# A graph network with attention and mixture of experts, on one core: the one-hots of keys and locals of a tile in one VectorE instruction

## What is computed

```python
xn = _layernorm(x)
agg = segment_sum(xn[dst], src, num_segments=3125)      # 53125 edges
y = agg + w * xn
h = relu(relu(relu(y @ W1.T) @ W2.T) @ W3.T)            # 256 -> 64 -> 32 -> 256
graph = h + xn
q, k, v = heads(xn)                                     # 8 heads of 32; q, k = elu + 1
mix = (q @ (k.T @ v)) / max(q @ sum(k), 1e-6)           # linear attention, per head
x = x + graph + (mix @ Wproj.T + bproj)
x = x + moe(_layernorm(x))                              # 8 experts, top 2, gelu; adds its input too
```

## Time and profile before

| | us |
|---|---|
| median of 3 runs | 431.22 (428.87 to 433.67) |
| the profiled execution | 430.48 |
| its span, first to last instruction | 428.8 |

### The profile page before, as it was taken

One profiled execution on the slowest core, in us unless ns is written; L12 is line 12 of the kernel. 1 busy time (PEld: TensorE's weight loads), 2 busy tenths in 40 slices (PEclk: granted clock), 3 DMA queues, 4 the chain that ended last, 5 costly groups with the idle time before them and its releaser, 6 DMA issues.

```text
span 428.8 us, 10052 instructions
## 1 busy us (share of the span) xinstructions
PE 404.5 (94%) x3141; PEld 318.8 (74%) x3141; DVE 311.2 (73%) x785; ACT 265.8 (62%) x676; POOL 183.5 (43%) x298
## 2 busy tenths in 40 slices
PE   4989899997999999999999999978999999999995
PEld 1767678776677777777755667854999998988894
DVE  3688858967899999999727653667688887655553
ACT  1756655575788888888824614441776766666663
POOL 4058969246100010001091114464456565655655
PEclk9899999999999999999999987577999999999999
DMA  8927310006589999999997961124465665467651
GB/s 211 194 70 255 90 26 8 1 2 125 106 152 172 172 175 167 179 184 189 167 215 227 308 224 63 65 81 120 151 190 188 187 210 159 140 202 207 186 177 38
DMA packets 111827, 64.11 MB, mean 150 GB/s; under 512 B 87985, under 2 KB 102202, under 8 KB 111646
## 3 DMA queue, kind: packets, MB, share of 16 engines
q1 hardware_dynamic: 104590, 48.14, 51.0%
q0 software_dynamic: 6368, 14.47, 9.6%
q10 hardware_dynamic: 816, 0.85, 0.8%
HBM read 24.00 MB, written 21.44 MB: 106 GB/s over the span
## 4 chain that ended last, share of the span: by engine, by line
PE 52%; POOL 12%; issue 11%; DMA 10%; DVE 10%; ACT 3%; SPq 1%; POOLq 0%; DVEq 0%
PE bank L1432 9%; PE bank L1381 8%; PE bank L1475 6%; POOL xs_next L653 5%; PE bank L1346 4%; PE bank L1444 4%; DMA region_a<-xs_next 4%; PE bank L1355 3%; POOL out L660 3%; DMA out<-region_a 3%; PE bank L1612 2%; PE bank L1594 2%; PE bank L1454 2%; DMA xs_next<-region_a 2%; POOL region_a L648 2%
## 5 line engine op out<-in xcount | busy, mean ns | idle before, releaser
L725 ACT CAST region_a<-bank 128x500 bf16<-128x500 f32 (+1 forms) x119 | 70.0, 673 | 14.8 <-PE bank L1381 14.8
L1681 PE MATMUL bank<-region_a,region_c 128*128 128x128 f32 x496 | 65.6, 275 | 0.0
L1692 PE MATMUL bank<-region_c,region_a 128*128 128x256 f32 x248 | 64.0, 380 | 0.0
L1681 PEld LDWEIGHTS bank<-region_a,region_c 128*128 128x128 f32 x496 | 60.3, 191 | 0.1
L1142 DVE COPY region_c<-region_w 128x1026 f32 x62 | 43.5, 701 | 19.2 <-issue 17.7
L605 POOL COPY wide<-den 125x256 f32<-125x256 f32 x25 | 13.0, 518 | 100.6 <-DVE den L1057 100.6
L1381 PE MATMUL bank<-region_a 128*128 128x125 bf16 x625 | 52.9, 219 | 1.5 <-ACT region_a L725 1.4
L1381 PEld LDWEIGHTS bank<-region_a 128*128 128x128 bf16 x625 | 42.2, 101 | 13.6 <-ACT region_a L725 3.2
L989 DVE TENSOR_TENSOR region_a<-iota,keys 128x3150 bf16<-128x3150 bf16 x25 | 44.9, 1796 | 5.4 <-PE bank L1381 5.4
L1304 DVE SCALAR_TENSOR_TENSOR region_a<-bank,region_a 128x256 f32<-128x256 f32 x62 | 30.0, 484 | 22.1 <-PE bank L1692 19.9
L815 ACT COPY region_a<-bank 128x256 f32<-128x256 f32 x62 | 23.1, 373 | 36.9 <-PE bank L1670 36.8
(11 more groups left out here) (239 smaller groups left out, 775.6 us busy)
## 6 DMA issues: line engine op xcount, KB each, us to landing
region_a<-xs_next SPq DMA_DIRECT2D x31, 259.0 KB, 2.9
region_w<-in_w SPq DMA_DIRECT2D x4, 1024.0 KB, 9.7
region_a<-xs SPq DMA_DIRECT2D x31, 131.0 KB, 2.4
rows<-in_x SPq DMA_DIRECT2D x5, 560.0 KB
xs_next<-null SPq DMA_DIRECT2D x8, 259.0 KB, 4.9
xs_next<-null SPq DMA_DIRECT2D x1, 1554.0 KB, 11.4
xs<-null SPq DMA_DIRECT2D x8, 131.0 KB, 3.1
region_q<-in_b SPq DMA_DIRECT2D x1, 1024.0 KB, 9.6
```

The source lines that it names most:

```text
L725: nc.scalar.copy(to, count_bank(n)[:, 0:w * TP].rearrange("p (c t u) -> p c t u", c=w, t=NT)).then_inc(adj_done, 1)
L1681: last = nc.tensor.matmul(hid_ps[c % 2][:, f * P:(f + 1) * P], wc[:, c % 3, k * D + f * P:k * D + (f + 1) * P], xT[:, c % 2, k * P:(k + 1) ...
L1692: last = nc.tensor.matmul(y_ps[c % 2][:, 0:D], hT[:, c % 2, f * P:(f + 1) * P], wc[:, c % 3, (2 + f) * D:(3 + f) * D], start=False, stop=( ...
```

## The change

The one-hots of both kinds get one buffer, `onehots[slot, kind, group, column]`, each row 128 columns apart, and keys and locals one buffer of pairs, stored tile by tile (keys of a tile, then locals of the tile). One function, `make_onehots(t, kinds)`, compares 126 columns of one kind or of both. In the loop over tiles it makes both kinds in one instruction of 50 rows of 126 columns; tiles 0, 1 and 2 are made one kind at a time in the old places. The last two columns of the locals' rows, which are no longer written by it, are set to zero once at the start. One semaphore stands for two. `region_a` grows by 48 words, and what lies behind the one-hots in it moves.

```diff
-        r = Region("region_a", GT * (KW + P) + 2 * NT * P + 2)
-        koh = r.take(P, 2 * GT * KW, BF16).rearrange("p (s c n) -> p s c n", s=2, c=GT)
-        loh = r.take(P, 2 * GT * P, BF16).rearrange("p (s c n) -> p s c n", s=2, c=GT)
+        r = Region("region_a", 2 * GT * P + 2 * NT * P)
+        onehots = r.take(P, 4 * GT * P, BF16).rearrange("p (s k c n) -> p s k c n", s=2, k=2, c=GT)
         adj = [r.take(P, NT * P, BF16).rearrange("p (t n) -> p t n", t=NT) for _ in range(2)]
-        r.take(P, 2)
...
-        keys = sb("keys", [P, NG, 2], BF16)
-        locs = sb("locs", [P, NG, 2], BF16)
+        pairs = sb("pairs", [P, NB * 5, 2, GT, 2], BF16)
+        keys, locs = pairs[:, :, 0, :, :], pairs[:, :, 1, :, :]
...
-                twice = keyf[:, lo:hi].rearrange("p (n a) -> p n a", a=1).to_broadcast([P, n, 2])
+                tiles = slice(lo // GT, hi // GT)
+                by_tile = "p (t c a) -> p t c a"
+                twice = keyf[:, lo:hi].rearrange(by_tile, c=GT, a=1).to_broadcast([P, n // GT, GT, 2])
                 nc.vector.scalar_tensor_tensor(
-                    locs[:, lo:hi, :], twice, -float(P),
-                    got.rearrange("p (n a) -> p n a", a=1).to_broadcast([P, n, 2]), ALU.mult, ALU.add)
-                nc.vector.tensor_scalar(keys[:, lo:hi, :], twice, unheld[:, 0:1], None, ALU.add
+                    locs[:, tiles, :, :], twice, -float(P),
+                    got.rearrange(by_tile, c=GT, a=1).to_broadcast([P, n // GT, GT, 2]), ALU.mult, ALU.add)
+                nc.vector.tensor_scalar(keys[:, tiles, :, :], twice, unheld[:, 0:1], None, ALU.add
                                         ).then_inc(keys_done, 1)
...
-            def key_onehots(t):
+            def make_onehots(t, kinds):
                 if t >= 2:
                     dve.wait_ge(chunk_ready, NBLK * (t - 1))
-                nc.vector.tensor_tensor(koh[:, t % 2, :, :].rearrange("p c (m u) -> p c m u", u=2), counting(KW),
-                                        columns(keys, t, KW), ALU.is_equal).then_inc(koh_done, 1)
-
-            def local_onehots(t):
-                if t >= 2:
-                    dve.wait_ge(chunk_ready, NBLK * (t - 1))
-                nc.vector.tensor_tensor(loh[:, t % 2, :, :].rearrange("p c (m u) -> p c m u", u=2), counting(P),
-                                        columns(locs, t, P), ALU.is_equal).then_inc(loh_done, 1)
-
+                n = len(kinds) * GT
+                kinds = slice(kinds[0], kinds[-1] + 1)
+                return nc.vector.tensor_tensor(
+                    onehots[:, t % 2, kinds, :, 0:KW].rearrange("p k c (m u) -> p (k c) m u", u=2),
+                    iota16[:, 0:KW].rearrange("p (a m u) -> p a m u", a=1, u=2).to_broadcast([P, n, KW // 2, 2]),
+                    pairs[:, t, kinds, :, :].rearrange("p k c (a u) -> p (k c) a u", a=1).to_broadcast([P, n, KW // 2, 2]),
+                    ALU.is_equal)
+
+            nc.vector.memset(onehots[:, :, 1, :, KW:P], 0.0)
             link(moments(0, J, 0))
...
-            key_onehots(2)
+            make_onehots(2, (0,))
             dve.wait_ge(ctx_turned, 1)
             nc.vector.tensor_copy(mout[:].rearrange("p c d -> p (c d)"), mix_ps[:]).then_inc(ctx_back, 1)
             invert(0)
-            local_onehots(2)
+            make_onehots(2, (1,)).then_inc(onehots_done, 1)
...
                 if 1 <= t < NT - 2:
-                    key_onehots(t + 2)
-                    local_onehots(t + 2)
+                    make_onehots(t + 2, (0, 1)).then_inc(onehots_done, 1)
                 divide(t)
...
                 if i == 0:
-                    pe.wait_ge(koh_done, t + 1)
-                    pe.wait_ge(loh_done, t + 1)
+                    pe.wait_ge(onehots_done, t + 1)
...
-                    last = nc.tensor.matmul(count_bank(n)[:, (c - lo) * TP:(c - lo + 1) * TP], loh[:, t % 2, c, :],
-                                            koh[:, t % 2, c, 0:TP], start=True, stop=True)
+                    last = nc.tensor.matmul(count_bank(n)[:, (c - lo) * TP:(c - lo + 1) * TP], onehots[:, t % 2, 1, c, :],
+                                            onehots[:, t % 2, 0, c, 0:TP], start=True, stop=True)
```

More of the change, by code:

```diff
@@ L150, in build @@
         assert r.at <= adjT_at + NT * P
-        r.restart(adjT_at - 2 - NT * P // 2)
+        r.restart(adjT_at - NT * P // 2)
         eq = r.take(P, 4 * TP).rearrange("p (s n) -> p s n", s=2)
         rq = r.take(P, 4 * TP).rearrange("p (s n) -> p s n", s=2)
-        assert r.at <= adjT_at - 2
+        assert r.at <= adjT_at
         r.restart()
@@ L317, in build @@
             "value_done", "held_done", "held_ready", "turned", "keys_done", "spill_known"))
-        pad_zeroed, wident_done, koh_done, loh_done, chunk_ready, adj_done = map(sem, (
-            "pad_zeroed", "wident_done", "koh_done", "loh_done", "chunk_ready", "adj_done"))
+        pad_zeroed, wident_done, onehots_done, chunk_ready, adj_done = map(sem, (
+            "pad_zeroed", "wident_done", "onehots_done", "chunk_ready", "adj_done"))
         turned_in = [sem(f"turned_in{s}") for s in range(2)]
@@ L1038, in _ @@
                     make_keys(t == 18)
[L1039 to L1046, removed]
+                if t in (19, 21):
+                    make_onehots((t - 19) // 2, (0,))
+                if t in (20, 22):
+                    make_onehots((t - 20) // 2, (1,)).then_inc(onehots_done, 1)
             def invert(t):
```

## The result

| | before | after |
|---|---|---|
| median, us | 430.09 (20 runs, 427.47 to 433.67) | 433.61 (20 runs, 428.54 to 435.48) |
| ratio | | 1.0059 (95%: 1.0032 to 1.0085) |
| the profiled execution: time, span | 430.48, 428.8 | 431.36, 429.6 |

By the ratio the kernel became slower by about 2.5 us, half a per cent; the ratio leaves out four executions of the changed kernel (435.09 to 435.48 us) that lie over 1.5% above its fastest, while the medians, 3.5 us apart, are of all 20.

The account below looks back on a forecast made before the run. TensorE, busy for 94% of the span, was taken to bound the kernel. The held copy (+1.70) and narrower locals (-0.02), other terms 0, on a base of 430.85 gave 432.5 us; range 430.0 to 435.2 us.

Parts of the forecast that it names:

- The bound: In the long loop TensorE sets the 4.67 us period; VectorE time saved there only lengthens its waits for TensorE's counts.
- a shrinking period: Sign against the prediction: if the loop's period of 4.67 us a tile shrinks, VectorE was in it.
- The merged instruction: Loop, 22 tiles: one instruction of 6300 columns for two saves VectorE 0.1 us each, 2.2 us, worth nothing in the sum.
- What the merge closes: Start of the loop: tile 3's merged one-hots hold GpSimd's copy of tile 1 longer, so the second spread comes later, +1.70 us.
- nothing moves: Rival: the copy's delay is of fixed size, or the copy wins against the first merged instruction; 430.8 us, chance 0.13.
- The lock in every tile: Rival: one-hots get ahead of GpSimd's copy in 22 tiles, 42 us slower, 473 us; the two slow rivals 0.03 together.
- Pair layout, locals, memset: Outside the long loop: keys written tile by tile 0 (up to 0.47 us loss), narrower locals 0.02 us earlier, memset hidden.
- Other addresses: TensorE's counts, key one-hots every 256 bytes instead of 252 and `adj` moved: taken as 0, bounds 3.2 us either way.
- The clock: Rival: TensorE's longer wait before `spread(1)` lowers the granted clock, 1.7 us more, 434.2 us; chance 0.11.
- The sum: Whole kernel: 430.85 us, the middle of four runs, + 1.68 = 432.5 us; within 1% of before at 0.89.

Follow-up runs that it names:

- the kernel with the filler: The changed kernel with eight matmuls of zeros put into TensorE's wait before the second spread; ratio to the kernel before 1.0048 (1.0016 to 1.0079), timed again 1.0040.

## Why the prediction was right, and where not

*The bound.* Right. TensorE sets the period; VectorE's 0.1 us a tile went into its waits, answered by 6.5 us after. I had said about 7.5; most of the difference is the period, which shrank by 0.04 us in each of 20 tiles. I had named a shrinking period as a sign that the prediction is wrong and VectorE sets it. The sign came, but not for that reason: the kernel with two instructions everywhere has the same 114.32 us.

*The merged instruction.* Right, in its size too: 3.36 us start to start after 3.45, 3.44 us long.

*What the merge closes.* Right. Forecast +1.70 us, from the second half of 3150 columns without its fixed part; measured +1.64 in the trace, which would be 0.01 below the lower end that I took (1.65). Removing that one merged instruction took it back. The rule of the Trainium skill that was weighed there (SBUF — State Buffer, "SBUF: two separate sides": a lock held for the whole instruction) is borne out by three lengths, 0.61, 1.86 and 3.50 us, as far as the whole length goes; that the two SBUF inputs are the reason, no run here shows. A fixed delay, the rival *nothing moves*, is refuted. The lock in every tile didn't come: the copies stand at 0.40 us beside `mix_add`, as argued from the earlier trace rows.

*Pair layout, locals, memset.* Right at zero: the keys' instruction takes 0.73 us as in the earlier trace rows, and TensorE waits 0.61 us for it, as it did.

*Other addresses.* The step that failed, a term that I left at 0 within bounds of 3.2 us either way. It is -0.88 us. I wrote that nothing in the trace pointed to it; in fact it is 0.04 us in the 25 matmuls of a tile, a difference that one piece of four with two decimals, as in the earlier trace rows, can hardly show.

*The clock.* I gave it 0.11 and 1.7 us, taken from the stretch at 10 us. It happened in one of three traces of the changed kernel and cost 3.15 us there. So its size was too low by almost half, and its chance probably too, by the mean clocks of all executions.

*The sum.* 432.5 us were forecast, +1.7 on a base of 430.85; the base came out at 430.09 and the changed kernel at 433.61, with a ratio that stands for +1.4 to +3.7 us. The forecast of a time within 1% of before, a little slower, held, and the held copy that I gave as the reason is the largest part that is shown; but the hit is also luck in part, since the term that I missed (-0.88) is made up for by the rest of about the same size or more that the clock, undersized, probably brings.

## What to carry to other kernels

Before two instructions of VectorE are made one, look at what GpSimd does beside them: the gap between the two may be where its operation gets in, and the first tiles of a pipeline, where a neighbouring instruction that keeps them apart is still missing, are where it shows. Where another engine sets the period, a saved instruction is worth nothing, and the whole effect of the change is in its side effects: here one held copy (+1.64 us) and the spacing of an operand's rows (-0.88 us). A short dependent copy belongs on the engine that made its input when that engine would otherwise lock out the other one: 0.29 us there replaced 3.50.

## What the runs showed of the hardware

- A GpSimd copy of 125x256 that takes 0.40 us alone takes 0.61, 1.86 and 3.50 us behind a VectorE compare of 756, 3150 and 6300 bf16 columns with two SBUF inputs that started 0.15 us ahead: 0.52 ns a column, which is the compare's own pace.
- Count matmuls of 128x125 bf16 take 0.04 us less in 25 when the rows of the streamed operand begin every 256 bytes instead of every 252.
- After 2.35 us of idle TensorE the granted clock fell in one of three traced executions of the same kernel, to 0.50 for the 4 us from 112 to 116 us and to 0.64 on the mean of the next 4, and cost 3.15 us. In the kernel with the filler it fell behind 1.08 us of idle time already (0.71 on the mean of 104 to 108 us).
